# Two attentions interleaved by units of eight heads, with each batch's experts moved into the next turn

## What is computed

```python
mod = (silu(c) @ wmod)                        # six rows per batch: sa, ca, ga, sb, cb, gb
h = layernorm(x) * (1 + ca) + sa
x = x + ga * attention1(h)                    # 16 heads of 16, causal, then o_proj
h = layernorm(x) * (1 + cb) + sb
x = x + gb * ffn(h)
# ffn: xn = layernorm(h) * ln_g + ln_b; attention2 over xn, 32 heads of 8, all keys; o = att @ wo + h
#      rows in 16 blocks of 256; block i goes through expert i % 8: gelu(o @ w1 + b1) @ w2 + b2
```

## Time and profile before

| | |
|---|---|
| median of 3 runs | 1743.81 us (1743.48 to 1747.54) |
| profiled execution, own time | 1751.3 us |
| its span, first to last instruction | 1749.4 us |
| busy: PE, DVE, ACT, POOL | 85%, 67%, 58%, 30% |
| mean granted clock of TensorE, of full speed | 0.973 |
| one turn of the main loop | 201.4 us |
| HBM traffic over the span | 96 GB/s |

### The profile page before, as it was taken

The page is one execution under the profiler, slowest core; times in us unless marked ns, Lnnn a source line. Parts: engine busy times, 40 slices in busy tenths (PEclk is TensorE's granted clock), DMA queues, the critical chain, the costliest instruction groups (busy, mean ns, idle before and its releaser), DMA issues.

```text
span 1749.4 us, 30247 instructions
## 1 busy us (share of the span) xinstructions
PE 1495.2 (85%) x10001; PEld 662.9 (38%) x10001; DVE 1166.8 (67%) x2989; ACT 1007.4 (58%) x2096; POOL 528.3 (30%) x1219
## 2 busy tenths in 40 slices
PE   5785789988999889988899889989899887979767
PEld 4333323344333533345333443335333442314315
DVE  6665589646976479755986469763896458775430
ACT  1252567755676457754676456764577555666571
POOL 4232335222433144222443235231352224200100
PEclk9697999999999999999999999999999999989999
DMA  6741334325235233422444333432443241222201
GB/s 190 200 104 39 108 116 125 99 65 140 79 89 137 76 110 119 107 76 82 126 107 120 88 103 94 100 103 76 131 125 98 65 109 50 84 53 60 82 1 60
DMA packets 136742, 170.48 MB, mean 97 GB/s; under 512 B 16968, under 2 KB 102280, under 8 KB 136592
## 3 DMA queue, kind: packets, MB, share of 16 engines
q1 hardware_dynamic: 130704, 164.17, 34.2%
q10 hardware_dynamic: 5888, 4.37, 0.9%
HBM read 110.67 MB, written 56.66 MB: 96 GB/s over the span
## 4 chain that ended last, share of the span: by engine, by line
PE 65%; DVE 17%; ACT 8%; issue 5%; DMA 2%; POOL 1%; SPq 1%; ACTq 0%; POOLq 0%; DVEq 0%
PE bank_out L1228 16%; PE bank_scores L1209 10%; DVE neg_max L1456 8%; PE bank_max L1180 7%; PE bank_side L1315 7%; PE bank_side L1143 6%; ACT probs L1002 5%; PE bank_side L1299 4%; PE bank_side L1153 3%; PE bank_scores L1299 3%; PE bank_side L1237 2%; PE bank_side L1271 2%; PE bank_side L1280 2%; DVE normed L1406 2%; PE bank_side L1118 1%
## 5 line engine op out<-in xcount | busy, mean ns | idle before, releaser
L1002 ACT ACTIVATE probs<-bank_scores 128x512 f32<-128x512 f32 (+3 forms) x1536 | 753.3, 545 | 403.6 <-PE bank_scores L1209 385.7
L1456 DVE TENSOR_REDUCE neg_max<-bank_max 128x1 f32<-128x512 f32 x1024 | 653.6, 683 | 164.8 <-PE bank_max L1180 159.9
L1209 PE MATMUL bank_scores<-q_stack,k_stack 64*128 64x512 bf16 (+3 forms) x2048 | 317.3, 346 | 92.2 <-ACT probs L1002 77.1
L1228 PE MATMUL bank_out<-probs,v_tile 128*9 128x512 f32 (+4 forms) x3072 | 367.7, 551 | 15.6 <-ACT out_raw L1016 12.4
L1180 PE MATMUL bank_max<-k_stack,q_stack 64*128 64x512 bf16 (+3 forms) x2048 | 316.2, 344 | 70.1 <-DVE neg_max L1456 35.9
L1453 DVE CUSTOM_DVE_ANT_0 bank_max<-bank_max,causal 128x384 f32<-128x384 f32 (+3 forms) x512 | 241.9, 515 | 107.6 <-PE bank_max L1180 104.8
L1209 PEld LDWEIGHTS bank_scores<-q_stack,k_stack 64*128 64x128 bf16 x2048 | 85.0, 93 | 365.0 <-issue 343.5
L869 POOL TENSOR_SCALAR_AFFINE_SELECT probs<-probs 128x512 f32<-128x512 f32 x128 | 80.9, 632 | 347.3 <-ACT probs L1002 347.3
L1180 PEld LDWEIGHTS bank_max<-k_stack,q_stack 64*128 64x128 bf16 x2048 | 105.6, 95 | 154.8 <-issue 107.5
L851 POOL CAST max_parts<-max_row 16x128 bf16<-16x128 f32 x96 | 28.4, 296 | 371.1 <-DVE max_row L1467 371.1
L1315 PE MATMUL bank_side<-w_out,hidden_T 128*128 128x256 f32 x512 | 118.8, 385 | 4.8 <-issue 3.7
(11 more groups left out here) (147 smaller groups left out, 1545.6 us busy)
## 6 DMA issues: line engine op xcount, KB each, us to landing
q_stack<-q_parts SPq DMA_DIRECT2D x124, 256.0 KB, 4.3
k_stack<-k_parts SPq DMA_DIRECT2D x122, 192.0 KB, 6.1
w_in<-in_L_ffn_w_dram SPq DMA_DIRECT2D x16, 1024.0 KB, 5.5
w_out<-in_L_ffn_w_dram SPq DMA_DIRECT2D x16, 1024.0 KB, 8.3
q_parts<-partsq SPq DMA_DIRECT2D x32, 384.0 KB, 2.6
k_parts<-partsk SPq DMA_DIRECT2D x32, 384.0 KB, 2.8
q_parts<-partsq SPq DMA_DIRECT2D x32, 256.0 KB, 2.9
k_parts<-partsk SPq DMA_DIRECT2D x32, 256.0 KB, 3.1
```

What stands on the lines that cost most here:

```text
L1002: nc.scalar.activation(probs[s % 2][:, head_at(k), q0:S], region[bank][:, q0:S], ACT.Exp, scale=float(WIDTH[a]) ** -0.5).then_inc(drained[ ...
L1209: ins = pe.matmul(region[to][:, q0:S], k_stack[buf][rows, at, kt * P:(kt + 1) * P], q_stack[buf][rows, at, q0:S], start=(i == 0), stop=last)
L1228: ins = pe.matmul(outb[32 * k:32 * k + WIDTH[a] + 1, q0:S], v_tile[a][:, kt, g * GROUP + k, :], probs[s % 2][:, k, q0:S], start=(kt == 0), ...
L1456: v.tensor_reduce(dst, region[bank], AX_X, ALU.max).then_inc(drained[bank], 1)
```

## The change

The section `loop` and `after` become one list `run`, written out for all batches.

- Order of steps: the first turn is as before (32 steps of attention 1 of batch 0, 16 of attention 0 of batch 2). In turns n = 1 to 5, sixteen steps of attention 1 of n, eight of attention 0 of n + 2, sixteen of attention 1, eight of attention 0.
- Experts of a batch run in the next turn, first expert at step 6, second at step 26, with pieces of the norms of other batches in the clusters. `expert_out` stands in quarters in slots of their own. The store of y is an item of its own (`store_y`), one or more slots later.
- Norm, queries and keys of attention 0 of batch n + 3 move to the end of turn n; its values are made at the next turn's start.
- The last two batches' attention 1 (64 steps) now also has the experts of batch 5 beside it, and those of batch 6 at steps 42 and 50.
- PSUM banks of `scores` and `maxima` rotate by the position in the whole list. `heads`, `gb_bc` and `x_res` get a second buffer; `b2_bc`, `max_rest` and `zeros` go (their work is done in place or in other tiles). `qk` goes by half of the features (`oc`) first, and its stores are counted for each half apart.

```diff
+    for n in range(1, BATCHES - 2):
+        one, two = steps_of_attention(n, 1), steps_of_attention(n + 2, 0)
+        main += one[:2 * UNIT_STEPS] + two[:UNIT_STEPS] + one[2 * UNIT_STEPS:] + two[UNIT_STEPS:]
+    return main + steps_of_attention(BATCHES - 2, 1) + steps_of_attention(BATCHES - 1, 1)
...
+def slot_of(first, n):
+    return SLOTS * (first + n // 10) + n % 10
...
+def cluster(b, j, under=((), ())):
+    items = [("gelu_table", b, j)]
+    for n in range(2):
+        items += [*in_pieces("expert_in", b, j, n), ("gelu", b, j, n)]
+    items += [*under[0], ("values_early",), ("maxima_early", 0), ("maxima_early", 1)]
+    for n in range(2, 4):
+        items += [*in_pieces("expert_in", b, j, n), ("gelu", b, j, n)]
+    return items + [*under[1], ("maxima_early", 2), ("maxima_early", 3)]
...
+def place_chain(plan, first, b, e):
+    place_units(plan, first, (23, 31), [("head_features", b, 0, 0), ("head_features", b, 0, 1)])
+    place_units(plan, first, (33, 41, 43, 53), out_items(b))
+    place_units(plan, first, (61, 61), layernorm_items(b, 1)[:2])
+    place_cluster(plan, first, 63, e, 0, norm_under(b, 1))
+    place_units(plan, first, (73, 81), [("ffn_input", b, 0), ("ffn_input", b, 1)])
+    place_expert_out(plan, first, (73, 81, 83, 83), e, 0, 0)
+    place_units(plan, first, (93, 101, 103, 103, 103, 103, 103, 131, 133), layernorm_items(b, 2))
+    place_expert_out(plan, first, (103, 111, 113, 123), e, 0, 1)
+    place_units(plan, first, (83, 132, 141), [("load_expert_in", e, 1), ("store_y", e, 0), ("load_expert_out", e, 1)])
+    place_units(plan, first, (141, 143), features_items(b, 2))
...
+def place_pass(plan, first, n):
+    place_units(plan, first, (1, 13, 93, 133), v_items(0, n + 2))
+    place_units(plan, first, (13,), [("bias_part", n, 0)])
+    place_chain(plan, first, n + 1, n - 1)
+    place_units(plan, first, (11, 83, 163, 251, 323, 403),
+                [("stacks", n + 2, 0), ("stacks", n, 4), ("stacks", n, 5), ("stacks", n + 2, 1), ("stacks", n + 1, 2), ("stacks", n + 1, 3)])
+    place_units(plan, first, (71, 123), [("load_residual", n + 2), ("load_mod", n + 2)])
+    place_units(plan, first, (153, 163, 171, 181, 191, 201, 211, 221), qk_items(1, n + 1))
+    place_units(plan, first, (193, 213), features_items(n + 1, 1))
+    place_units(plan, first, (231, 241, 253, 273), v_items(1, n + 1))
...
+    place_cluster(plan, first, 263, n - 1, 1, norm_under(n + 3, 0) if more else ((), ()))
...
+        place_units(plan, first, (281, 283), features_items(n + 3, 0))
+        place_units(plan, first, (293, 333, 373, 383, 393, 403, 411, 441), qk_items(0, n + 3))
+    place_expert_out(plan, first, (303, 311, 313, 323), n - 1, 1, 0)
+    place_expert_out(plan, first, (343, 351, 353, 363), n - 1, 1, 1)
+    place_units(plan, first, (373, 391, 401), [("store_y", n - 1, 1), ("load_expert_out", n, 0), ("load_gate", n + 1)])
+    place_units(plan, first, (413,), [("keep_v", n + 1)])
+    place_units(plan, first, (423, 431), [("head_features", n, 1, 0), ("head_features", n, 1, 1)])
+    for mc, at in ((0, 451), (1, 461)):
+        place(plan, slot_of(first, at), in_pieces("ffn_sum", n, mc), 0)
...
             def load_gate(b, f):
-                wait(sp, y_made, 2 * b + 1)
+                wait(sp, y_made, 2 * b - 1)
...
-            def expert_out(b, f, j, k):
-                if k == 0:
-                    return
+            def store_y(b, f, j):
                 wait(sp, y_made, 2 * b + j + 2)
```

More of the change, by code:

```diff
@@ L222, in place_experts, with place_last_experts @@
+def place_last_experts(plan, b, at):
+    place(plan, at, [("head_features", b, 1, 0), ("head_features", b, 1, 1)], SLOTS)
+    place_at(plan, (at + 2 * SLOTS, at + 3 * SLOTS), [("ffn_sum", b, 0), ("ffn_sum", b, 1)])
+    for j, first in ((0, at + 4 * SLOTS), (1, at + 8 * SLOTS)):
+        plan.setdefault(first, []).extend(cluster(b, j))
         if j == 0:
-            items.append(("load_expert_in", off, 1))
-        place_at(plan, (start + 2, start + 2 * SLOTS), [("expert_out", off, j, k) for k in range(2)])
+            plan[first].append(("load_expert_in", b, 1))
+        place_at(plan, (first + 2, first + 2 * SLOTS), [("expert_out", b, j, k) for k in range(2)])
+        plan[first + 2 * SLOTS].append(("store_y", b, j))
@@ new lines, in main_order, with place_cluster, place_expert_out @@
+def main_order():
+    return steps_of_attention(0, 0) + steps_of_attention(1, 0) + steps_of_run()
+POSITION = {step: n for n, step in enumerate(main_order())}
+EXPERT_BANKS = {}
+def place_cluster(plan, first, n, b, j, under=((), ())):
+    slot = slot_of(first, n)
+    place(plan, slot, cluster(b, j, under), 0)
+    step = slot // SLOTS + 2 * T_STEPS * HEADS[0] // GROUP
+    EXPERT_BANKS[b, j] = "scores%d" % ((GROUP * step + 2) % 3)
+def place_expert_out(plan, first, numbers, b, j, k):
+    for part, n in enumerate(numbers):
+        place(plan, slot_of(first, n), [("expert_out", b, j, k, part)])
@@ new lines, in place_units @@
+def place_units(plan, first, numbers, items):
+    for n, item in zip(numbers, items, strict=True):
+        place(plan, slot_of(first, n), [item])
+def place_chain(plan, first, b, e):
[9 more added lines that the diff above has]
+    place_units(plan, first, (141, 143), features_items(b, 2))
@@ L334, in sections @@
-    place(beside, n1 + 3, [("keep_v", 1)])
-    place_experts(beside, 0, n1 + 15)
-    place(beside, n1 + 48, [("load_gate", 1), ("load_expert_in", 1, 0), ("load_expert_out", 1, 0)])
-    place(beside, n1 + 56, [("bias_part", 1, 0), ("bias_columns", 1)])
-    place_experts(beside, 1, 2 * n1 + 3)
-    ahead = steps_of_attention(0, 1)[LEAD:] + steps_of_attention(1, 1)
-    after = attention(steps_of_attention(0, 1) + steps_of_attention(1, 1), one_each(ahead), beside, handed)
-    after = [item for item in after if item != ("keep_x", 2)]
@@ L342, in sections @@
-    return (("start", start), ("scale", scale), ("first", first), ("second", second), ("before", before), ("loop", loop), ("after", after))
+    place_first_pass(beside)
+    for n in range(1, BATCHES - 2):
+        place_pass(beside, PASS * n, n)
+    place_tail(beside, PASS * (BATCHES - 2))
+    main = steps_of_run()
+    run = attention(main, one_each(main[LEAD:]), beside, handed)
+    return (("start", start), ("scale", scale), ("first", first), ("second", second), ("before", before), ("run", run))
@@ L559, in build @@
         y_stored = [sem("y_stored%d" % j) for j in range(2)]
-        main_names = ("before", "loop", "after")
+        main_names = ("before", "run")
         def number(fill):
@@ L1082, in _ @@
         def _(pe):
[L1084 removed]
+            pe.wait_ge(const_made, 6)
             def turn_weight(i, bank):
```

360 lines of the change are left out of this document (179 added, 181 removed).

## The result

The changed kernel takes 1751.17 us (median of 10 runs, 1747.05 to 1756.28), the kernel before, run beside it, 1746.51 us (10 runs, 1743.48 to 1751.42). The ratio is 1.0031, with a 95% interval from 1.0015 to 1.0046: 5 us slower, where I had forecast 113 us less. None of the rivals' times came out either.

A forecast was written before the change was run, and what follows sets the result against it. VectorE was taken to bound the non-causal part, neither it nor ScalarE the rest; evenly mixed, TensorE would set the turn. First turn -22, five turns -77, tail -14 made -113 us: 1631 us, range 1580 to 1700.

The forecast's parts named there:

- The clusters stay, two a turn, and switch ScalarE's table as before, so the switches cost nothing new: Expert input clusters in turns 1 to 5: ScalarE's table switches were to add no cost over the kernel before.
- The output items come in quarters of 0.91 us, one or two a slot, so the chain behind them goes: Expert output items: quarters instead of 3.65 us whole were to remove the serial scores, exponentials and values behind them.
- Of the 12 us I keep 4: Of 12 us lost in a turn's last 16 steps before, at clusters and output items, 4 were to remain.
- For the lumps within a stretch I take 7.5: Allowance per interleaved turn for uneven work within its six eight-step stretches: 7.5 us on top of 174.6.
- The demand, 172.7 us a turn: TensorE's work in a middle turn, summed from start-to-start spacings; spread evenly, it alone would set the turn, near 173 us.
- The stretch of 28.1 us in the earlier trace: Check of the spacing count on eight steps of the kernel before: counted 28.4 us, measured 28.1, TensorE never idle.
- Rival A: TensorE's busy time, 181.1 us a turn, is its real demand: turn 192.6 us, kernel 1677 us; chance 0.17.
- VectorE's 0.91: VectorE busy at most 0.91 of the time, so eight steps need 26.3 us, setting two of six stretches.
- But norms and maxima now lie under them: Clusters in interleaved turns: VectorE was to have norms and maxima to do there; part of keeping 4 of 12 us.
- First turn: Keeps its order, loses both experts, gains batch 3's queries, keys and norm: 180 us, 22 less (12 to 28).
- tail: Last 64 steps, with batch 5's experts added: 250 us, 14 less than 263.9 (30 less to 5 more).
- rival D: SP's in-order queue stalls maxima stores, 7.17 us each; at four stalls a turn, 1774 us, slower; chance 0.07.

The follow-up runs named there:

- Experiment 1: Changed kernel with each expert's first output item whole, right behind its cluster, instead of in four quarters: 1730.05 us, ratio 0.9878 to the kernel before.
- experiment 3: Kernel before, with each expert's first output item, whole as it was, placed two slots later: 1785.41 us, ratio 1.0213.
- experiment 7: Changed kernel with the edits of Experiment 1 and experiment 2, and each expert's second output item whole too: 1711.96 us, ratio 0.9793.
- Experiment 10: Changed kernel with eight small unused identity products into the side bank behind each cluster: 1735.34 us, ratio 0.9916 to the kernel before.
- experiment 2: Changed kernel with side items moved one or two slots, off those of maxima transposes and normalise: 1722.08 us, ratio 0.9846 to the kernel before.
- experiment 12: experiment 6 with the non-causal row maximum over only 128 of 512 keys, so the output differs: 1670.53 us, ratio 0.9552 to the kernel before.
- experiment 11: experiment 6 with the norms' pieces moved out of the clusters into slots around them: 1687.55 us, ratio 0.9649 to the kernel before.
- experiment 6: The repaired kernel: changed kernel with the edits of Experiment 1 and experiment 2, and another second PSUM bank for the clusters: 1685.46 us, ratio 0.9641.
- experiment 8: experiment 6 with a tiny exponential right behind each cluster's last gelu, loading the table early: 1686.26 us, ratio 0.9639 to the kernel before.

## Why the prediction was wrong

**The step that failed** is in "What is still lost": "The clusters stay, two a turn, and switch ScalarE's table as before, so the switches cost nothing new", with "The output items come in quarters of 0.91 us, one or two a slot, so the chain behind them goes." The load is the same 1.28 us; what covered it was the whole output item, which I had down as the cause of the loss. I took from the earlier trace rows that scores, exponentials and values ran one behind the other after an output item, and not that 3.65 us of TensorE's work had lain over ScalarE's drain and load before that. Experiment 1 gives the cover back (-27 us), experiment 3 takes it from the kernel before (+37), experiment 7 shows that the quarters are right for the item that covers nothing (18 us). "Of the 12 us I keep 4" failed with it: the switches cost more than before, and not less.

**The clock was no term of my sum.** The two clusters' groups have 0.93 in the row where all of the earlier trace rows has 1.00. Experiment 10 leaves the waits and mends the clock alone: 20 us, where the whole cover is worth 27. So most of what the cover was worth is the clock, 1.6 us a fall, and not the wait itself, 0.6 at most. Falls also come elsewhere in the changed kernel, as in the causal group that waits for the side bank (19.8 us at 0.91 in the third interleaved turn, 18.2 at 1.00 in the fourth).

**"For the lumps within a stretch I take 7.5"** took a place in the list as free of cost as long as each stretch's sum fitted. A side item next to `max_rows` or `normalise` waits for VectorE to empty the one side bank, 1.02 and 1.28 us in the rows of experiment 2, and the scores behind it wait too. In the kernel before, whose projections stand elsewhere, the like waits were 5.2 us in all, and I carried that over to other slots. Experiment 2: 32 us. The two errors together are 60 of the 120 us between 1631 and 1751, and none of my bounds held them.

**The demand, 172.7 us a turn, was short by 5 to 8.** This is argued from spacings and busy time; no experiment isolates it. Three terms were mis-sized, all counted from spacings. I took 0.23 us for each pair. That holds where the next is of the same kind; the pair of maxima that stands ahead of an fp32 product has 0.31 (1042.30 to 1042.61 us in the changed kernel, and 376.94 to 377.26 before, ahead of an input item); at two of them in each of 32 steps that is up to 0.08 x 64 = 5 us. A quarter of an output item has 1.06 (1060.80 to 1061.86), not 3.65 / 4: 16 x 0.15 = 2.4 us. The other way, 0.365 us is about right for a causal pair of maxima but too much for one of scores, which has four lengths from 0.12 us (84.51 to 84.63 in the kernel before) over 0.34 (561.03 to 561.37) to 0.44, mean 0.28: 32 x 0.08 = 2.6 us too much. With all three the sum is 177.5 us. The stretch of 28.1 us in the earlier trace rows, where I counted 28.4, tested the count at one place only, and one with causal maxima, so that the pairs of 0.31 weren't in it. From the other side, a turn with two quartered items fewer has 181.1 us busy at a clock of 1.00 (experiment 1, third interleaved turn), but a record runs on for up to 0.16 us beyond the place where the next could start, which counts as busy ahead of each of some 35 waits a turn; the true demand lies between the two numbers. Rival A's reading (181.1) was nearer to it than mine. The Trainium skill, Perfetto Trace Analysis, section "Identifying the Most-Contended Engine", which I weighed there, calls matmul busy time no good measure of how close a kernel is to roofline; as an upper bound of this stream's demand it was within some 4 us a turn.

**VectorE's 0.91** set two stretches of each turn in my sum. It isn't the limit in interleaved turns (experiment 12); in the first turn's order it is at least part of it (7.5 us). That the even mix frees TensorE from waits for maxima was right (35.9 to 7.0 us); what it is worth was not: 17 us in the changed kernel and at most 8 in the repaired one. "But norms and maxima now lie under them" counted for nothing (experiment 11).

**First turn and tail.** The first turn was forecast rightly in kind, -16.8 for -22. The tail was forecast at 250 and took 270.8: it has four clusters with the same uncovered load; with both repairs and the bank it is 261.4. The short demand would account for most of the rest, by estimate: 56 steps with maxima at 2 x 0.08 make 9 us.

**What held.** SP doesn't stall behind stores (rival D): waits of the scores for `max_parts` go from 8.1 us to 0.3 in the rows above. The last 49 us are the same chain. The prologue's -5.1 us I can't assign; it is between 218 and 223 us in all kernels made from the changed one, 226.7 in experiment 3, so it belongs to the change, but I didn't take it apart.

**The account.** A middle turn at 205.4 where 186 was forecast, in TensorE's busy and idle time: two falls of the clock are 3.2 us; busy time without them is 181.5 for the 172.7 that I put down as demand (8.8); idle time is 20.7 for 13.3 (7.4). Repaired, the clock costs nothing, busy time is 180.4 and idle time 14.2. What those 14 us consist of is not settled: on TensorE's timeline of experiment 6 they are some 34 waits of 0.2 to 0.8 us, most of them for exponentials and for VectorE's part of a side item, and no experiment took them apart.

## What to carry to other kernels

Before splitting or moving a long item for its own cost, look at what ScalarE and VectorE do during it: a block that seems to cause a chain can be the cover of the chain ahead of it, and the split belongs only where there is none. Look at the granted clock of the groups too: here useless products in TensorE's stand won 20 of the 27 us that the whole cover won. Where one PSUM bank serves all side work, the order of neighbouring items in it is worth as much as the balance of the stretches, so count each item with the one that it follows. And test a count made from spacings on several stretches, with busy time plus idle time as its other side, before letting it overrule the busy row.

## What the runs showed of the hardware

- A stand of about 3 us on TensorE, with one pair of products in it, costs again afterwards in 12 of 14 places. The values behind it last 1.89 us for 1.04, and the window's granted clock, between the two levels of 1.2 and 2.4 GHz, is 0.93 over 25.5 us. 0.07 x 25.5 = 1.8 us, near the 1.6 by which the same group is shorter where the clock stayed at 1.00, and that eight useless products win back in experiment 10. In experiment 3, with the stand at another place of another kernel, the item behind it lasts 4.67 us for 3.72.
- A switch of ScalarE's table takes 1.30 us from its start to the start of the next activation (1058.44 to 1059.74). The Trainium skill, ScalarE: Activation LUTs, section "What ACT_TABLE_LOAD costs", gives the load 1283 ns, as the row has it, and about 1380 ns of drain on top. No such drain shows here: in experiment 8 the load starts at 438.33 us, 0.02 behind the end of the last gelu, and the next activation at 439.62. ScalarE's idle 0.60 us ahead of the load in the changed kernel is a wait for scores.
- A pair of bf16 products over half of the rows has 0.23 us where the next is such a pair too, and 0.31 ahead of a full fp32 product.
